# One kernel, two edits: the expert stage's register loads, loops and queue order, and attention scores in two stacked passes

## The reference

```python
x = x + 0.5 * moe(layernorm(x))             # 8 experts, top 2, GELU, a layernorm per expert
x = x + decay_attention(layernorm(x))
x = x + 0.5 * moe(layernorm(x))
x = x + 0.5 * fp4_ffn(layernorm(x))
x = x + bias_attention(layernorm(x), w_q, w_k, w_v, w_o, table)   # 16 heads of 64
x = x + 0.5 * fp4_ffn(layernorm(x))
```

```python
h = gelu(z @ w1[e] + b1[e]); res = z + h @ w2[e] + b2[e]
y = layernorm(res) * gamma[e] + beta[e]
```

```python
q, k, v = z @ w_q, z @ w_k, z @ w_v
p = softmax(q @ k.T + position_bias)      # no scaling
out = concat_heads(p @ v) @ w_o
```

## Time and profile before

| | |
|---|---|
| median of 3 runs (lowest, highest) | 3229.51 us (3228.45, 3241.72) |
| the profiled execution: time, span | 3240.09 us, 3238.0 us |
| mean granted TensorE clock | 0.903 of full speed |
| busy PE, DVE, ACT, POOL over the span | 74%, 70%, 57%, 43% |
| experts of M0, experts of M1 | some 350 us each |
| attention A1, from the first scores | 1278 us |

### The profile page before, as it was taken

One profiled execution on the slowest core, in us unless ns is written; L12 is line 12 of the kernel. 1 busy time (PEld: TensorE's weight loads), 2 busy tenths in 40 slices (PEclk: granted clock), 3 DMA queues, 4 the chain that ended last, 5 costly groups with the idle time before them and its releaser, 6 DMA issues. The chain is left out here.

```text
span 3238.0 us, 66865 instructions
## 1 busy us (share of the span) xinstructions
PE 2386.1 (74%) x17707; PEld 1919.1 (59%) x17707; DVE 2265.8 (70%) x8247; ACT 1857.2 (57%) x4874; POOL 1401.3 (43%) x1366
## 2 busy tenths in 40 slices
PE   2217888384226787307868999999999999999587
PEld 2217676363225676305655877777777777778365
DVE  4325766685433666577977888888888888888697
ACT  2114444252213344235637988888888888889464
POOL 3553555302563555405532444444444444444365
PEclk9999999696558999758988999999999999999799
DMA  4133333312114333340000000000000000000000
GB/s 151 40 67 93 98 99 95 100 39 87 40 50 100 97 99 95 94 122 1 0 27 4 5 4 4 4 4 4 4 4 4 4 4 4 4 4 5 6 20 27
DMA packets 141736, 138.32 MB, mean 43 GB/s; under 512 B 17012, under 2 KB 127412, under 8 KB 140772
## 3 DMA queue, kind: packets, MB, share of 16 engines
q1 hardware_dynamic: 118932, 95.46, 9.8%
q0 software_dynamic: 17408, 35.82, 3.5%
q10 hardware_dynamic: 5200, 4.84, 0.5%
HBM read 59.31 MB, written 44.24 MB: 32 GB/s over the span
## 5 line engine op out<-in xcount | busy, mean ns | idle before, releaser
L2088 POOL TENSOR_TENSOR p_prob<-p_prob,p_inverse 128x512 f32<-128x512 f32 x512 | 533.3, 1042 | 797.0 <-DVE p_inverse L1912 797.0
L2005 ACT ACTIVATE p_prob<-p_neg,p_neg_max 128x256 f32<-128x256 f32 x1024 | 508.8, 503 | 40.2 <-DVE p_neg_max L1906 40.2
L1916 DVE SCALAR_TENSOR_TENSOR p_probT<-p_t_ps,p_probT 128x512 f16<-128x512 f32 x512 | 353.0, 689 | 195.1 <-ACT p_probT L2011 135.6
L883 ACT ACTIVATE p_e_hT<-p_e_h_ps,p_b 128x256 f32<-128x256 f32 x576 | 230.9, 474 | 352.9 <-PE p_e_h_ps L832 216.0
L997 POOL DMA_INDIRECT results_by_token<-p_e_result,p_e_slot x288 | 285.2, 990 | 309.6 <-DVE p_e_result L943 234.2
L706 POOL DMA_INDIRECT rows_by_expert<-p_r_z,p_r_target x256 | 249.4, 974 | 371.5 <-DVE p_r_z L561 258.2
L1906 DVE CUSTOM_DVE_ANT_0 p_neg<-p_s_ps,top_bias 128x256 f32<-128x256 f32 x1024 | 388.3, 416 | 0.8 <-ACT p_prob L2005 0.6
L2011 ACT ACTIVATE p_probT<-p_t_ps 128x512 f16<-128x512 f32 x512 | 304.9, 596 | 71.2 <-PE p_t_ps L2156 69.5
L841 PE MATMUL p_e_o_ps<-p_w,p_e_hT 128*128 x2304 | 308.2, 289 | 35.4 <-issue 22.7
L841 PEld LDWEIGHTS p_e_o_ps<-p_w,p_e_hT 128*128 128x128 f32 x2304 | 285.5, 201 | 55.9 <-issue 55.9
L2156 PE MATMUL p_t_ps<-top_ident,p_prob 128*128 128x128 f32 x2048 | 308.8, 273 | 7.0 <-POOL p_prob L2088 7.0
(11 more groups left out here) (266 smaller groups left out, 6157.3 us busy)
## 6 DMA issues: line engine op xcount, KB each, us to landing
p_e_affine<-p_affine SPq DMA_DIRECT2D x144, 192.0 KB
p_e_z<-rows_by_expert SPq DMA_DIRECT2D x144, 129.0 KB, 2.2
p_got<-results_by_token SPq DMA_DIRECT2D x64, 256.0 KB, 2.9
results_by_token<-p_e_result,p_e_slot POOLq DMA_INDIRECT x288
p_r_w<-in_w SPq DMA_DIRECT2D x2, 2048.0 KB, 7.6
p_w<-in_w SPq DMA_DIRECT2D x2, 2048.0 KB, 11.8
rows_by_expert<-p_r_z,p_r_target POOLq DMA_INDIRECT x256
p_reversed<-bias_by_distance ACTq DMA_DIRECT2D x2, 2048.0 KB, 17.1
```

What stands on the lines that cost most here:

```text
L1916: v.scalar_tensor_tensor(probT[k % 2][:, 1, :, :], t_ps[k % 2][:], PROB_SCALE, probT[k % 2][:, 0, :, :], ALU.mult, ALU.subtract).then_inc( ...
L2005: ins = act.activation(prob[k % PROBS][:, t, :], neg[k % 2][:, t, :], ACT.Exp, bias=neg_max[k % 2][:, t:t + 1], scale=-1.0, accum_out=tota ...
L2088: pool.tensor_tensor(prob[k % PROBS][:], prob[k % PROBS][:], inverse[k % PROBS][:].unsqueeze(2).to_broadcast([P, SEQ_TILES, SEQ]), ALU.mult)\
```

## The change

**Attention.** The products `a` are gone. Queries and keys are projected with w_q and w_k (two heads of 64 to a projection), so a quad needs 2 projections for q, 2 for k and 4 for v: as many as before, in the same slots (`FIRST_BANK` through `act_ps`, `SECOND_BANK` through `v_ps`). A head's parts lie in 64 partitions. SP moves them with DMAs within SBUF into `stacked`, which holds for each head the query's high part over its low part, and the key's high part twice. One matmul over 128 rows then gives high x high plus low x high, and a second over 64 rows, straight from `qkT`, gives high x low. Per quad SP issues 16 DMAs of 64 partitions x 1 KB (8 for each pair of heads), behind waits for `act_taken` and `v_taken`. PE waits for all 8 of a pair (`moved`) at the pair's first scores, which are those of slot 5 and slot 7 in the quad before; the pairs' keys are projected in slots 1 and 3. The start of A1 splits w_q and w_k directly, after all the statistics.

**Experts.** Registers are loaded with one call for several blocks (two on SP, up to four on PE and ACT) and without assertions. ACT's loop body covers two sets. POOL adds b2 before `give_back` and copies the slots after it, and SP waits for `slot_ready` too before it loads rows. PE's next four experts are read between an `up` and a `turn`, where before each was read ahead of a `down`. After the loop DVE finishes set 34 before it takes the residual of set 35. In the Newton step of the square root a `tensor_tensor` became a `scalar_tensor_tensor`.

```diff
-    chain.link(v.tensor_tensor(t, y, y, ALU.mult))
+    chain.link(v.scalar_tensor_tensor(t, y, 1.0, y, ALU.mult, ALU.mult))
...
+        def load_values(table, kind, highest):
+            _, values = nc.values_load_multi_w_load_instructions(
+                table, engines=[kind], min_val=0, max_val=highest,
+                skip_runtime_bounds_check_because="counted up from zero in whole blocks and clamped where the table is made")
+            return values
+
+        def experts(kind, n, sets):
+            first = n * SET + EXPERTS_AHEAD
+            return load_values(w["expert_of"][0:1, bass.ds(first, sets * SET)], kind, EXPERTS - 1)
... SP, before load_rows(n + 3)
                             sp.wait_ge(zb_ready, n)
                             sp.sem_inc(carried, 1)
+                            sp.wait_ge(slot_ready, n)
+                            sp.sem_inc(carried, 1)
... PE
+            for n in range(SETS):
+                following, pair = pair[:SET], pair[SET:]
+                for b in range(SET):
+                    down(n, n % 2, b, now[b])
+                    if n + 1 < SETS:
+                        up(n + 1, b, following[b])
+                    if b == 0 and not pair and n + 2 < SETS:
+                        pair = experts(mybir.EngineType.PE, n + 2, min(2, SETS - n - 2))
+                    if n + 2 < SETS:
+                        turn(n + 2, b, (n + 2) // RING, (n + 2) % RING)
+                now = following
... ACT
-            set_rings(act, ring)
+            pair(0)
+            loop_groups(act, 1, SETS // 2 - 1, pair)
+            pair(SETS // 2 - 1)
... DVE, after the loop
+            roots(0, 1)
+            normalise(SETS - 2, SETS // RING - 1, RING - 2)
             residual(SETS - 1, RING - 1)
-            roots_of_pair()
-            normalise(SETS - 2, SETS // RING - 1, RING - 2)
+            roots(1, 2)
             normalise(SETS - 1, SETS // RING - 1, RING - 1)
... POOL
+                    if behind(j, q, 1):
+                        add_b2(n + 1, *nth_in_ring(j, q, 1))
                     if behind(j, q, -2):
                         give_back(n - 2, (q - 2) % RING)
                     if behind(j, q, 1):
-                        take(n + 1, *nth_in_ring(j, q, 1))
+                        take_slots(n + 1, *nth_in_ring(j, q, 1))
... bias_attention
+FIRST_BANK = ((Q, 0), (Q, 1), (V, 0), (V, 2))
+SECOND_BANK = ((K, 0), (K, 1), (V, 1), (V, 3))
...
+            def move(of, pair, i, g):
+                here, there_ = qkT[g % 2], stacked[g % 2]
+                first, second = slice(0, D_HEAD), slice(D_HEAD, P)
+                for h, own in enumerate((first, second)):
+                    parts = (HIGH, LOW) if of == Q else (HIGH, HIGH)
+                    for part, to in zip(parts, (first, second) if h == 0 else (second, first)):
+                        sp.dma_start(there_[to, of, pair * 2 + h, :], here[own, part, of, pair, :]).then_inc(moved[of][pair], 16)
+
+            def stack_quad(i, g):
+                if not (first_group(i) and g < 2):
+                    sp.wait_ge(s_done, i * GROUP_UNITS + (g - 1) * UNITS)
+                    sp.sem_inc(carried, 1)
+                for pair in range(QUAD_PAIRS):
+                    sp.wait_ge(act_taken, g_ready(i, g, pair))
+                    sp.sem_inc(carried, 1)
+                    move(Q, pair, i, g)
+                    sp.wait_ge(v_taken, v_number(i, g, pair) + 1)
+                    sp.sem_inc(carried, 1)
+                    move(K, pair, i, g)
... scores
+                if b == 0 and hd % 2 == 0:
+                    for of in (Q, K):
+                        pe.wait_ge(moved[of][pair], (i * QUADS + (g + 1)) * 64)
...
-                    ins = three_passes(s_ps[k % 2][:, t, :], (gT[g % 2][:, 0, hd, rows], gT[g % 2][:, 1, hd, rows]),
-                                       (keys[:, 0, toks], keys[:, 1, toks]))
+                    pe.matmul(s_ps[k % 2][:, t, :], stacked[g % 2][:, Q, hd, rows], stacked[g % 2][:, K, hd, toks], start=True, stop=False)
+                    ins = pe.matmul(s_ps[k % 2][:, t, :], qkT[g % 2][half, HIGH, Q, pair, rows], qkT[g % 2][half, LOW, K, pair, toks],
+                                    start=False, stop=True)
... start of A1, DVE
             for n in range(QUADS):
                 norms.raw(v, n * (TILES // QUADS), TILES // QUADS, x_res)
-                v.wait_ge(a_kept, 2 * n + 1)
-                v.scalar_tensor_tensor(a_low[:, a_heads(n), :], a_bank(n), A_SCALE, a_high[:, a_heads(n), :], ALU.mult, ALU.subtract).then_inc(a_kept, 1)
+            for of in (Q, K):
+                v.wait_ge(qk_split, 2 * of + 1)
+                v.scalar_tensor_tensor(wqk_low[:, of], wqk[:, of], A_SCALE, wqk_high[:, of], ALU.mult, ALU.subtract).then_inc(qk_split, 1)
```

More of the change, by code:

```diff
@@ L396 @@
 RING = 4
+EXPERTS_AHEAD = 2
 def sparse_buffers(nc):
@@ L780, in load_affine @@
             def load_affine(n, q):
-                for b in range(SET):
-                    e = expert(sp, n, b)
+                for b, e in enumerate(experts(mybir.EngineType.SP, n, 1)):
                     sp.dma_start(affine[q][:, b, :, :], w["affine"][:, bass.ds(e, 1), :, :].rearrange("p e a d -> p (e a) d"))\
@@ L845, in down @@
                     ins.then_inc(o_done, 1)
[L847 to L860 removed]
             for b in range(SET):
                 turn(0, b, 0, 0)
+            now = experts(mybir.EngineType.PE, 0, 1)
+            pair = experts(mybir.EngineType.PE, 1, 2)
             for b in range(SET):
[L865 removed]
+                up(0, b, now[b])
                 turn(1, b, 0, 1)
[L867 to L868 removed]
+            for n in range(SETS):
[9 more added lines that the diff above has]
+                now = following
         @block.scalar
@@ L885, in hidden, with pair, there_is @@
                     ins.then_inc(h_ready, 1)
-            def ring(j):
-                for q in range(RING):
-                    n = j * RING + q
+            def pair(j):
+                chosen = experts(mybir.EngineType.Activation, j * 2 + 1, 2 if there_is(j, 2) else 1)
+                for q in range(2):
+                    n = j * 2 + q
                     for b in range(SET):
-                        if behind(j, q, 1):
-                            hidden(n + 1, b)
-                        if behind(j, q, 2):
+                        if there_is(j, q + 1):
+                            hidden(n + 1, b, chosen[q * SET + b])
+                        if there_is(j, q + 2):
                             keep_high(n + 2, b)
+            def there_is(j, n):
+                return not isinstance(j, int) or 2 * j + n < SETS
             act.preload_act_table_set("gelu_and_others")
@@ L989, in take, with take_slots @@
                                    affine[q][:, :, B2, :].unsqueeze(2).to_broadcast(shape), ALU.add).then_inc(zb_ready, 1)
+            def take_slots(n, nth, q):
+                if not early(n, RING):
+                    pool.wait_ge(returned[q % 2], (nth * (RING // 2) + q // 2 - 1) * SET_RETURNS)
+                    pool.sem_inc(carried, 1)
+                pool.tensor_copy(slot[q][:], z[q][:, :, D:ROW].bitcast(U32).rearrange("p t o -> p (t o)")).then_inc(slot_ready, 1)
             def give_back(n, q):
@@ L1765, in bias_attention @@
         keyT = m.sb("keyT", [P, 2, GN], F16)
-        gT = [m.sb(f"gT{b}", [P, 2, QUAD, GN], F16) for b in range(2)]
+        qkT = [m.sb(f"qkT{b}", [P, 2, 2, QUAD_PAIRS, GN], F16) for b in range(2)]
+        stacked = [m.sb(f"stacked{b}", [P, 2, QUAD, GN], F16) for b in range(2)]
         val = [m.sb(f"val{b}", [P, 2, GT, QUAD * D], F16) for b in range(2)]
@@ L1789, in bias_attention @@
                                              for key in ("o_done", "o_kept", "o_turned", "o_added"))
-        a_done, a_kept, b_done, b_kept = m.sem("a_done"), m.sem("a_kept"), m.sem("b_done"), m.sem("b_kept")
+        qk_split, b_done, b_kept = m.sem("qk_split"), m.sem("b_done"), m.sem("b_kept")
+        moved = [[m.sem(f"{key}_moved{pair}") for pair in range(QUAD_PAIRS)] for key in ("q", "k")]
+        carried = m.sem("carried")
         high_ready, key_ready = m.sem("high_ready"), m.sem("key_ready")
@@ L1798, in bias_attention, with kept @@
         OUT_SCALE = 1.0 / (PROB_SCALE * VALUE_SCALE)
+        HIGH, LOW = range(2)
+        def kept(g, part, use):
+            of, n = use
+            return (val[g % 2][:, part, n, :], VALUE_SCALE / (Z_SCALE * B_SCALE)) if of == V else \
+                (qkT[g % 2][:, part, of, n, :], QK_SCALE / (Z_SCALE * A_SCALE))
         def last_group(i):
@@ L1884, in keep_keys, with group @@
                 sp.dma_start(keyT[:], zT[:]).then_inc(key_ready, 16)
-            loop_groups(sp, 0, GROUPS, keep_keys)
+            def move(of, pair, i, g):
[16 more added lines that the diff above has]
+                    move(K, pair, i, g)
+            def group(i, ahead):
+                keep_keys(i)
+                for g in range(1, QUADS):
+                    stack_quad(i, g)
```

(12 more changed lines are left out.)

165 lines of the change are left out of this document (74 added, 91 removed).

## The result

The changed kernel takes 3253.42 us (median of 4 runs, 3253.28 to 3259.13), the kernel before beside it 3228.98 (3227.76 to 3241.72): ratio 1.0071, 95% interval 1.0044 to 1.0099. The forecast was 3093, its range 3040 to 3145 and its chance of slower 0.03.

The account below looks back on a forecast made before the run. PE was taken to bound attention, busy 1247 of 1278 us. Against the profiled 3240.1 us, -91 - 6.5 - 32 - 7 = -136.5 gave 3103.6; with the median 10.6 us lower, 3093, range 3040 to 3145.

Parts of the forecast that it names:

- Scores: Attention on PE: two matmuls fewer in each of 512 units, 0.218 us each unit, 111.6 us saved in all.
- rival D: Attention scores: a 64-row matmul between 128-row ones costs double, eating the 0.218 us per unit; total 3205, chance 0.04.
- Who is next: Attention, per group: PE stays longest at 70.7 us, DVE 68.5, ACT 65.4; 1 us more waiting, 16 us over 16 groups.
- rival A: Attention: DVE and ACT set the pace, the group stays at 77 us, total 3141; chance 0.14.
- Moves: Attention, SP's 16 DMAs per quad: 0.465 us an issue, 0.3 us a group, 5 us in all, bounds 0 and 16.
- rival C: Attention: SP can't issue the moves in time; 0.91 us an issue eats the whole 136 us; chance 0.04.
- SP's long loop body: Attention: SP's new loop body could stand 4.3 us at its branch, covered by slack; cost 0, up to 60 us without.
- the hole of DVE: Attention: DVE's hole of 4.3 us at its loop's branch stays in every group.
- Start of A1: Before the first scores: statistics no longer wait for the first bank of `a`; -6.5 us, bounds -7 and 0.
- Experts: Expert stages: shorter register reads cut waits for "issue" and z, 65 us exposed; half taken, -32, bounds 0 and -65.
- The -7 for b2 and the tail: End of both expert stages: no DVE wait for b2, set 34 normalised earlier; -3.5 us each, bounds 0 and -6.
- B': Experts: they gain all 65 us and the clock rises from 0.93 towards 1; total 3040, chance 0.10.

Follow-up runs that it names:

- e4: Changed kernel with the two score passes in reversed order for the second half of the rows (two changes of rows per unit, not four): 2989.32 us, ratio 0.9663.
- e3: Changed kernel with the second score pass also over 128 rows, same DMAs, waits and number of matmuls: 2928.96 us, ratio 0.9473 to the kernel before.
- e7: Kernel before with one of its three score passes over 64 rows instead of 128, no moves: 3442.44 us against 3250.25, ratio 1.059.
- e11: The same kernel as e3, run again on a slow chip beside e12: 3104.84 us, ratio 0.9546 to the kernel before.
- e12: e3 with 60 idle semaphore increments ahead of ACT's work in A1, moving its attention loop to place 1082: 3097.7 us, ratio 0.952 to the kernel before.
- e1: Kernel before with only the attention part of the change, old experts: 3177.87 us, ratio 1.0274.
- e6: Changed kernel unedited, run again on a slow chip: 3271.42 us, ratio 1.0068 to the kernel before.
- e13: New experts with old attention, SP alone reading each register by its own load with assertion: 3021.08 or 3019.12 us (order not stated), ratio 0.975 to the kernel before.
- e14: New experts with old attention, PE and ACT reading each register by its own load with assertion: ratio 0.9741 to the kernel before.
- e15: New experts with old attention, nothing undone, reference for e13 and e14 on a fast chip: 2990.39 us, ratio 0.9651 to the kernel before.
- e16: Kernel before with 4 idle semaphore increments ahead of DVE's work in A1, its attention loop at place 2551: 3061.05 us, ratio 0.9884.
- e10: New experts with old attention, POOL in its old order and SP not waiting for the slots, slow chip: ratio 0.9725 to the kernel before.

## Why the prediction was wrong, step by step

*Scores: wrong, and this decided the sign.* The step that failed is "64 rows cost nothing extra there". It took the latency of a 64-row matmul among matmuls of its own kind, and that is right (e4: 0.11 between the two). But the change puts 64-row matmuls between 128-row ones, and there the step between the starts is what counts. Four changes at 0.10 us are 0.41 a unit against a gain of 0.218: 512 x (2.59 - 2.40) = 97 us lost instead of 112 won (e3, e4 and e7 show that it is the change of rows). The rival D named this mechanism with a chance of 0.04 and priced only the two entries into 64 rows, not the two ways back, so that it ended at 3205. No row of attention in the trace of before could have warned, since A1's 64-row matmuls stand among themselves; the rule of the Trainium skill quoted above could, though it has no price, and the forecast did not weigh it.

*Who is next, and rival A: right that PE stays the longest, seen only in e3, with the waits too small.* With PE's unit at 2.18 a group takes 73.6 us, where the forecast had 70.7 + 1.3 of waiting and A had 77: 26 us more over sixteen groups. With ACT's hole moved it is 72.7.

*Moves and rival C: small in the changed kernel by luck.* An issue takes 0.596 us instead of 0.465, well below C's 0.91. The changed kernel waited 9.4 us in all instead of 5, but with a unit of 2.59 us in place of the 2.18 that the forecast reckoned with. In e3, at 2.18, it is 21.0 us behind the start's 7.2, above the upper bound of 16. Part of it goes with ACT's hole: from 1700 us to 2850 and 2840 e11 has 17.4 us of it and e12, without the hole, 9.7. SP's long body brought nothing on PE's path.

*SP's long loop body, and the hole of DVE: wrong.* The forecast cited the fetch rule and concluded "both holes come at the branch, and the sum stays". It took DVE's hole as a part of the loop. It is a matter of the place, and the expert edits ahead of it moved the body from 2548 to 2574 and the hole away: 77.2 instead of 79.7 us a group with the old attention. In the changed kernel, which PE bounds, it would have cost about 1 us a group (84.8 in e1 against 83.8). The 16 us of waiting that the forecast charged for it have no counterpart.

*Start of A1: half right.* The statistics did come 6 us earlier: from their first to `p_shift` 23.4 us instead of 29.3 (1617.14 to 1640.56 against 1676.69 to 1706.03). But the first quad's moves have no work beside them:

```profile
1665.45 0.37 PE L2217 MATMUL p_s_ps<-p_stacked 128*128 128x256 f16 x1 [7.02 <-DMA p_stacked<-p_qkT]
```

It is the first score matmul of A1 in the changed kernel's timeline of PE: 7.0 us, a term that the forecast did not have. It priced the moves in the steady state only.

*Experts: right in kind, 19 us short.* -57.8 against -39, and -46 on the chip of e6. The reads were the cause, as said, and PE's "issue" went. What was mis-sized is their worth: the forecast took half of 65 us. Undone on SP they cost 31 us (e13), on PE and ACT 29 (e14), where the forecast had 26 at most for "issue". The wait for z did not go to near 0, though: in e15 it is 14.8 and 17.3 us beside 15.1 and 15.5 with the old experts (e16), in stages that are 33 us shorter. The -7 for b2 and the tail doesn't show on a slow chip (e10). And the clock, which B' had rising, fell here from 0.94 and 0.91 to 0.90 and 0.88.

With the measured terms in place of the forecast's, -57.8 - 0.6 + 68.6 + 3.1 = +13.3, and 3240.1 + 13.3 = 3253.4, the profiled 3253.46.

## What to carry to other kernels

Where PE is the bound, count how often the number of rows changes from one matmul to the next, not only how many matmuls there are: here each change cost nearly as much as a whole 256-column matmul (0.10 against 0.11 us), and filling the other 64 rows won some 158 us, reckoned from the parts. Price an operation by its step in the neighbourhood in which it will stand; a latency among its own kind says nothing about that. And before taking a hole at a loop's branch as given, look where the body stands in the engine's instruction stream: any edit ahead of it can bring the hole or take it away, and four idle increments were worth 1.2%.

## What the runs showed of the hardware that was not expected

- A change between 64-row and 128-row matmuls costs 0.10 us each way at the full clock, and the weight load isn't hidden there (0.20 to 0.22 us from start to start instead of 0.11).
- The hole at a loop's branch goes with the place of its body: for DVE 4.3 us at 2548, two waits of 2.2 and 1.6 us at 2546, none from 2551 to 2574, one of 2.1 us at 2747; for ACT 1.4 to 1.5 us at 1023 and 1029, none at 1082, 1099, 1435 and 1441.
- A load of four registers takes 0.332 us on PE's queue, one of a single register 0.304.
- Chips differ by 4 to 5% for this kernel, nearly all of it ahead of attention, and SP's instructions show it: an assertion takes 18 ns at most on one and up to 0.74 us on another. Why is open.
